# Attention and a feed-forward block on one core: the first images' norms, gelus, convolutions and sums of squares inside the last attention image, and the second image's products ahead of the first maxima

## The reference, cut to what matters

```
h = gelu(rmsnorm2d(x, norm1_w))
x = x + conv1x1(h, conv_w, conv_b)
h = rmsnorm2d(x, norm2_w)
h = gelu(conv1x1(h, ffn_w1, ffn_b1))
x = x + conv1x1(h, ffn_w2, ffn_b2)
```

## Time and profile before

| | us |
|---|---|
| median of 3 runs | 1737.22 (1735.89 to 1737.3) |
| profiled execution, its own time | 1736.72 |
| its span in the trace | 1734.7 |
| PE busy | 1680.9 (97%) |
| DVE busy | 1456.1 (84%) |
| ACT busy | 1368.5 (79%) |
| POOL busy | 337.7 (19%) |
| mean granted TensorE clock | 0.977 |

### The profile page before, as it was taken

How to read it: one execution, slowest core, us unless ns; L and a number is a source line. 1 busy time by engine, 2 the same in 40 slices (tenths; PEclk the granted TensorE clock), 3 DMA queues, 4 the chain that set the end, 5 groups by cost and what they waited for, 6 DMA issues and landing times.

```text
span 1734.7 us, 33327 instructions
## 1 busy us (share of the span) xinstructions
PE 1680.9 (97%) x12402; PEld 677.8 (39%) x12402; DVE 1456.1 (84%) x2414; ACT 1368.5 (79%) x2480; POOL 337.7 (19%) x411
## 2 busy tenths in 40 slices
PE   4999999999999999999999999999999997699999
PEld 2333333333333333333333333333333332355555
DVE  4899999999999999999999999999999991455552
ACT  1288888888888888888888888888888887566664
POOL 4101111111111111111111112121211011322220
PEclk8599999999999999999999999999999998799999
DMA  6133333333333333333333333333333301233332
GB/s 118 24 45 57 56 59 56 59 56 59 54 60 54 60 55 60 55 60 53 61 53 62 53 62 52 50 52 51 51 50 53 51 18 48 87 99 107 105 109 73
DMA packets 58817, 106.17 MB, mean 61 GB/s; under 512 B 33184, under 2 KB 33952, under 8 KB 58656
## 3 DMA queue, kind: packets, MB, share of 16 engines
q1 hardware_dynamic: 56352, 95.66, 32.3%
q10 hardware_dynamic: 2304, 8.39, 1.2%
HBM read 34.48 MB, written 9.06 MB: 25 GB/s over the span
## 4 chain that ended last, share of the span: by engine, by line
PE 91%; DVE 4%; DMA 1%; SPq 1%; POOL 1%; issue 1%; ACT 1%; DVEq 0%; ACTq 0%; POOLq 0%
PE psum L619 30%; PE psum L590 26%; PE psum L603 12%; PE psum L685 6%; PE psum L528 4%; DVE maxes L877 4%; PE psum L657 2%; PE psum L658 2%; PE psum L659 2%; PE psum L565 2%; PE psum L520 2%; PE psum L702 1%; DMA k_stack<-k_low 0%; POOL rms_out L500 0%; PE psum L540 0%
## 5 line engine op out<-in xcount | busy, mean ns | idle before, releaser
L877 DVE TENSOR_REDUCE maxes<-psum 128x1 f32<-128x512 f32 x2048 | 1277.4, 683 | 107.7 <-PE psum L590 105.6
L794 ACT ACTIVATE probs<-psum 128x512 f32<-128x512 f32 x2048 | 1109.3, 597 | 194.0 <-PE psum L603 168.9
L590 PE MATMUL psum<-k_stack,q_stack 62*128 62x512 f32 x2048 | 772.3, 458 | 8.3 <-DMA k_stack<-k_low 4.7
L603 PE MATMUL psum<-q_stack,k_stack 64*128 64x512 f32 x2048 | 752.9, 451 | 1.0 <-ACT probs L794 0.9
L619 PE MATMUL psum<-probs,values 128*32 128x256 f32 (+1 forms) x6912 | 620.2, 431 | 0.5 <-ACT probs L794 0.5
L590 PEld LDWEIGHTS psum<-k_stack,q_stack 62*128 62x128 f32 x2048 | 317.2, 188 | 523.6 <-DVE maxes L877 434.8
L603 PEld LDWEIGHTS psum<-q_stack,k_stack 64*128 64x128 f32 x2048 | 305.0, 185 | 14.3 <-ACT probs L794 9.0
L619 PEld LDWEIGHTS psum<-probs,values 128*32 128x32 f32 x6912 | 136.1, 108 | 310.6 <-issue 231.1
L417 POOL CAST parts<-neg_max 128x16 fp32r<-128x16 f32 x64 | 12.7, 198 | 534.9 <-DVE neg_max L856 534.9
L685 PE MATMUL psum<-probs,inv_den 128*128 128x512 f32 x256 | 116.5, 598 | 0.0
L803 ACT ACTIVATE probs<-psum,params_sb 128x512 f32<-128x512 f32 x128 | 82.2, 686 | 20.9 <-PE psum L659 14.8
(11 more groups left out here) (82 smaller groups left out, 998.2 us busy)
## 6 DMA issues: line engine op xcount, KB each, us to landing
q_stack<-q_high SPq DMA_DIRECT2D x128, 128.0 KB, 3.7
k_stack<-k_high SPq DMA_DIRECT2D x128, 128.0 KB, 5.2
x_sb<-in_x SPq DMA_DIRECT2D x16, 512.0 KB, 7.0
q_stack<-q_low SPq DMA_DIRECT2D x64, 128.0 KB, 6.3
k_stack<-k_low SPq DMA_DIRECT2D x64, 128.0 KB, 7.0
q_stack<-rows SPq DMA_DIRECT2D x512, 2.0 KB
attn<-raw SPq DMA_DIRECT2D x128, 64.0 KB, 2.3
inv_den<-inv_den_rows SPq DMA_DIRECT2D x128, 64.0 KB, 2.3
```

What stands on the lines that cost most here:

```text
L590: nc.tensor.matmul(psum[:, BANKS + tile % BANKS, :], q_stack[used, place, p, chunk % 4, chunk // 4, :], k_stack[used, place, p, HALF * key ...
L603: nc.tensor.matmul(psum[:, tile % BANKS, :], k_stack[used, place, p, 128 * chunk:128 * chunk + 128], q_stack[used, place, p, :, t, :], sta ...
L794: nc.scalar.activation(probs[:, tile % 8, :], psum[:, tile % BANKS, :], ACT.Exp, scale=SCALE).then_inc(probs_ready, 1)
L877: nc.vector.tensor_reduce(maxes[:, chunk // 4, j, 4 * p + chunk % 4, key_half:key_half + 1], psum[:, BANKS + max_tile(u, s, k) % BANKS, :] ...
```

## The change

- **Start.** PE makes all four q and k products and both value pieces of an image in one go (`prologue_image`), for the first and for the second image ahead of unit 0's maxima, in `FIRST_BANKS`. The group mean waits for the value copies. DVE makes the low parts of the first image (`first_rests`), which POOL made.
- **Breaks.** `has_job` makes a step broken only where there is a job.
- **Unit 30** (image 15, first half): POOL squares images 0 and 1, PE sums them at step 5 in bank 7, ACT copies the sums; SP loads all layer 1 weights and spreads the norms of images 0 and 1 (chain 0).
- **Unit 31.** `lead_in(0)` after step 4: norms 1 of images 0 and 1, splits of `wconv` and `w1`, their four gelus. PE convolves image 0 in step 5. `lead_in(1)` after step 6: sums of images 2 and 3, convolution of image 1. `lead_in(2)` after step 9: sums of the convolved images 0 and 1, then norm 1 of image 2 and norm 2 of image 0 on DVE. `lead_in(3)` after the last weighing: denominators of image 15, gelu and split of image 2.
- **After it.** `refine(0)` has its own order: hidden(0,0), convolution of image 2, hidden(0,1), sums, both down products. The projection of image 15 follows it (`project_last`, banks 3 and 4). `refine(1)` to `refine(15)` keep theirs.
- Storage: separate `sums`, `first_weights` for four small weights and later `w2`, a DRAM row pair for each of the first chains.

The core of the diff, common part and run:

```diff
-LAST_PROJ = (0, 15)
+
+
+FIRST_SUMS, FIRST_CONV = (0, 5), (1, 5)
+CHAINS = 3
+
+FIRST_BANKS = ((0, 1, 2, 3), (0, 1, 2, 6))
+PROLOGUE = len(FIRST_BANKS)
...
-            return {None: range(STEPS), 0: range(2), 1: range(2, 7), 2: range(7, 13), 3: range(13, STEPS)}[part]
...
+            return {None: range(STEPS), 0: range(5), 1: range(5, 7), 2: range(7, 10), 3: range(10, STEPS)}[part]
 
         def qk_bank(c, n):
-
-            return psum[:, n, :] if c == 0 else misc
...
+        def prologue_image(b, half, s):
+
+            return b + 2 if half == 1 and s == 2 and 0 <= b + 2 < PROLOGUE else None
...
+        def run(eng, slot, lead_in, refine, project_last=lambda: None):
...
             slot(IMAGES - 1, 1, 0)
-            for part in range(2):
+            for part in range(3):
                 slot(IMAGES - 1, 1, 1, part)
-            refine(-4)
-            slot(IMAGES - 1, 1, 1, 2)
-            refine(-3)
+                lead_in(part)
...
             slot(IMAGES - 1, 1, 1, 3)
             slot(IMAGES, 0, 0, 0)
-            activate(-3)
...
+            lead_in(3)
             refine(0)
...
+            project_last()
+            for c in range(1, IMAGES):
                 refine(c)
```

SP and POOL:

```diff
+                if half == 0 and b == IMAGES - 1:
+                    sp.dma_start(wconv[:, :], d["wconv"]).then_inc(ffn_weights_in, 16)
+                    sp.wait_ge(split_done, 2 * IMAGES)
+                    sp.dma_start(w1, d["w12"][:, 0:HIDDEN]).then_inc(ffn_weights_in, 16)
+                    sums_in(0)
+                if half == 0 and has_image(b - 1) and part is None:
+                    denominators(b - 1)
+                if half == 0 and b == IMAGES - 1:
+                    rms_rows(0)
+                    sp.wait_ge(pv_done, (u - 1) * STEPS + STEPS)
+                    sp.wait_ge(scores_ready, u * TILES)
+                    spread(0, 0, inv_rms1, inv1_in)
+                    spread(0, 1, inv_rms2, inv2_in)
+                    sp.dma_start(w2, d["w12"][:, HIDDEN:2 * HIDDEN]).then_inc(ffn_weights_in, 16)
...
+            def lead_in(part):
+                if part == 1:
+                    sums_in(1)
+                    rms_rows(1)
+                    sp.wait_ge(normed1_ready, 1)
+                    spread(1, 0, inv_rms1, inv1_in)
+                if part == 2:
+                    sums_in(2)
+                    rms_rows(2)
+                    sp.wait_ge(normed1_ready, 2)
+                    spread(2, 0, inv_rms2, inv2_in)
+                if part == 3:
+                    sp.wait_ge(normed1_ready, 3)
+                    spread(1, 1, inv_rms1, inv1_in)
+                    sp.wait_ge(normed2_ready, 1)
+                    spread(2, 1, inv_rms2, inv2_in)
+                    denominators(IMAGES - 1)
...
+                if c == 0:
+                    return
...
+                if half == 0 and b == IMAGES - 1:
+                    pool.wait_ge(split_done, 2 * IMAGES)
+                    pool.wait_ge(v_ready, 2 * IMAGES)
+                    square_of(0, square1)
+                    square_of(1, square2)
...
+                if half == 0 and b == IMAGES - 1:
+                    inverse_rms(0)
...
+            def lead_in(part):
+                if part == 0:
+                    pool.wait_ge(sums_ready, 1)
+                    square_of(2, square1)
+                    square_of(3, square2)
+                if part in (1, 2):
+                    inverse_rms(part)
+                if part == 3:
+                    normalise(IMAGES - 1)
...
```

PE:

```diff
+                if b == IMAGES - 1 and (half, s) == FIRST_SUMS:
+                    pe.wait_ge(ffn_setup, 3)
+                    pe.wait_ge(proj_taken, (b - 1) * NT)
+                    pe.wait_ge(first_squares, 2)
+                    sum_squares(square1, square2, 7)
...
+                if prologue_image(b, half, s) is not None:
+                    pe.wait_ge(hid_ready, c + 1)
+                    at_least(pe, qk_full, c * 4)
+                    for n in range(4):
+                        qk_product(c, n)
+                    at_least(pe, gn_var, c + 1)
+                    values_of(c, 0)
+                    pe.wait_ge(v_full, c * 2 + 1)
+                    values_of(c, 1)
+                if half == 1 and s in QK_STEPS and c >= PROLOGUE and has_image(c):
...
+            def has_job(b, half, s):
+                at = (half, s)
+                if at in (LAST_K, *VALUES):
+                    return PROLOGUE <= b + 1 < IMAGES or at == FIRST_SUMS and b == IMAGES - 1
+                if at in (GROUP_MEAN, GROUP_VAR):
+                    return has_image(b + 2)
+                if at in PROJ:
+                    return 0 < b < IMAGES
+                return half == 1 and s in QK_STEPS and PROLOGUE <= b + 2 < IMAGES
...
-                    broken = s in SIDE_STEPS[half] or b == IMAGES and (half, s) == LAST_PROJ
+                    broken = has_job(b, half, s)
+                    if b == IMAGES - 1 and (half, s) == FIRST_CONV:
+                        for k in range(3):
+                            scores(u, 2 * parity + half, s, k)
+                        weigh_before(u, parity, half, s, 0, HALF)
+                        pe.wait_ge(max_taken, UNITS * TILES)
+                        pe.wait_ge(weights_split, 1)
+                        convolve(0, 0)
+                        convolve(0, 1)
+                        scores(u, 2 * parity + half, s, 3)
+                        continue
                     middle = 2 if s % NK == 1 and not broken else 1
...
-                        if k == 1 and broken:
+                        if k == 1 and (broken or b < 0):
...
+            def lead_in(part):
+                if part == 1:
+                    pe.wait_ge(first_squares, 4)
+                    pe.wait_ge(sums_taken, 1)
+                    sum_squares(square1, square2, SUMS_BANK)
+                    convolve(1, 0)
+                    convolve(1, 1)
+                if part == 2:
+                    pe.wait_ge(sums_taken, 2)
+                    pe.wait_ge(conv_squares, 2)
+                    sum_squares(square1, square2, SUMS_BANK)
...
+                if c == 0:
                     pe.wait_ge(weights_split, 2)
                     pe.wait_ge(probs_ready, UNITS * TILES)
+                    pe.wait_ge(proj_taken, (IMAGES - 1) * NT)
+                    hidden(0, 0)
+                    convolve(CONV, 0)
+                    convolve(CONV, 1)
+                    hidden(0, 1)
+                    sums_of(0)
                     pe.wait_ge(acc_taken, UNITS * NT)
+                    pe.wait_ge(ffn_weights_in, 48)
+                    down(0, 0)
+                    down(0, 1)
+                    return
+                if c == 1:
                     pe.wait_ge(proj_taken, IMAGES * NT)
...
+            def project_last():
+                b = IMAGES - 1
+                pe.wait_ge(attn_ready, b + 1)
+                pe.wait_ge(conv_taken, (CONV + 1) * NT)
+                for t in range(NT):
+                    nc.tensor.matmul(psum[:, CONV_BANKS[t], :], wp[:, :], attn[:, HALF * t:HALF * t + HALF],
+                                     start=True, stop=True).then_inc(proj_ready, 1)
...
```

ACT, then DVE:

```diff
+                if prologue_image(b, half, s) is not None:
+                    for n in range(4):
+                        take_qk(b + 2, n)
+                    for part in range(2):
+                        take_values(b + 2, part)
...
+                if b == IMAGES - 1 and (half, s) == FIRST_SUMS:
+                    act.wait_ge(sums_ready, 1)
+                    act.wait_ge(pv_done, u * STEPS)
+                    nc.scalar.copy(sums, misc).then_inc(sums_taken, 1)
...
+            def lead_in(part):
+                if part == 0:
+                    activate(0)
+                    activate(1)
...
+            def refine(c):
+                if c == 0:
+                    activate(CONV)
+                    gelu_hidden(0, 0)
+                    square_in_front(0)
+                    square_behind(0)
+                else:
+                    square_in_front(c)
+                    store(c - 1)
+                    square_behind(c)
                     gelu_hidden(c, 0)
-                if has_image(c + FIRST - 1) and not is_first(c + FIRST - 1):
-                    activate(c)
-                if has_image(c):
-                    gelu_hidden(c, 1)
+                    if has_image(c + FIRST - 1):
+                        activate(c + FIRST - 1)
+                gelu_hidden(c, 1)
+                if c == 0:
+                    activate(FIRST - 1)
...
+                if b == -2 and half == 1 and s == 15:
+                    first_rests(0, q_full, q_high, q_low)
+                    first_rests(1, k_full, k_high, k_low)
...
+            def lead_in(part):
+                if part == 0:
+                    dve.wait_ge(stack_in, UNITS * (16 * STACK_DMAS))
+                    dve.wait_ge(added, 2 * NT)
+                    norm_in_front(0)
```

(24 more changed lines are left out.)

362 lines of the change are left out of this document (182 added, 180 removed).

## The result

| kernel | median, us | lowest to highest | executions |
|---|---|---|---|
| before | 1737.26 | 1735.89 to 1737.68 | 4 |
| with the change | 1713.83 | 1712.49 to 1714.98 | 4 |

What follows compares the result with a forecast made beforehand. The prediction took the kernel as PE-bound except for two holes, at the start and late. Terms -2.0 - 1.5 + 7.2 - 23.2 = -19.5 against 1736.7 gave 1717.2, plus 0.5 for the median: 1717.7 us, range 1710 to 1727.

Steps and rivals of the forecast that it cites:

- A: Start: second image's products and value pieces moved before the first maxima; -2.0 us, bounds +1 and -4.
- C: Last unit: table loads, gelus, convolutions and sums added on ScalarE and PE; +7.2 us, bounds +5 and +11.
- B: Units 29 and 30: jobless steps no longer broken, first sum of squares added; -1.5 us, bounds -3 and +1.
- D: From the last attention matmul to `refine(1)`: reordered work shortens this stretch; -23.2 us, bounds -25 and -20.
- moving the two rests ... nothing: Start: moving the splits' low parts from GpSimd to VectorE gains nothing, as PE no longer waits for the stacks.
- the wait for the rows of maxima: Start: first scores would newly wait for the rows of maxima to land; +1.2 us.
- The -3.5 for the jobs that leave the first slot: Slot 0: one product (counted 1.5 us) and two value pieces at 1.0 each go; -3.5 us.
- Rival 2: Start gives nothing: first maxima at 42 and the rows late; 1719.7 to 1720.7 us, chance 0.15.
- Rival 1: Last unit: clock holds in the gelu gap, and units 29 and 30 give their bound; 1715 us, chance 0.2.
- Rival 5: Last unit: clock falls in the gelu gap and stays down until `refine(1)`, so slower; 1746 us, chance 0.03.
- Rival 3: Last unit: table switches have a drain beside the load, 2.8 us more; 1720.5 us, chance 0.08.
- Rival 4: A chain of norms is late, or PE waits inside the last unit; 3 to 5 us, 1721 to 1723, chance 0.1.

Runs made afterwards that it cites:

- rests_back: The changed kernel with the low parts of the first image's q and k formed on GpSimd again instead of VectorE; median 1717.92 us.
- breaks_back: The changed kernel with steps broken by their number again, whether or not they have a job; median 1719.98 us.
- change_again: The changed kernel run once more with nothing edited; median 1715.30 us.
- swap: The changed kernel with VectorE splitting the third gelu output ahead of the reciprocal of the last denominators; median 1710.49 us.
- all3: The changed kernel with GpSimd's later squares, twelve useless matmuls before the first convolution, and the third gelu's split ahead of the last reciprocal; median 1709.76 us.
- two_more_loads: all3 plus one unused single-column gelu on ScalarE in the last unit, forcing one more pair of table switches; median 1712.85 us.

## Why the prediction was right, and where it was not

The sum was right within its range, and a good part of that is luck: two errors of opposite sign met. A gave 5.2 more than forecast, beyond its bound of -4, and C cost 3.2 more. The mechanisms of B and D held. Of the 3.9 us between forecast and median, 2.2 are the sum's (-21.7 for -19.5), 0.5 was added for a median above the profiled execution, and 1.2 is that here the profiled execution was the slowest of its four.

**A: -2.0 forecast, -7.2 measured.** Three steps of it failed. First, "moving the two rests ... nothing": GpSimd, not SP, is what the second image's norm waits for once its products stand in front; rests_back prices it at 2 to 3 us. The prediction looked at the stacks, for which TensorE no longer waits, and not at what else stands behind the rests on their engine. Second, the wait for the rows of maxima, +1.2, isn't there: first maxima to first score is 31.74, all of it VectorE's pace (53 maxima at 0.60). Third, the unbroken steps of units 0 and 1, 1.6 to 3 us by breaks_back, were counted nowhere. The products and value pieces cost less than I took (5.39 for 6.8; the granted clock was back before 33), which gives the rest of the 3.0 us by which the first maxima came before 40.5. The -3.5 for the jobs that leave the first slot looks right only because it stands beside that third error: from the first score to unit 28 the change has -4.2, but breaks_back, where the jobs are gone and the breaks stay, has -2.1 (1254.1 for 1256.2).

Rival 2, that the start gives nothing, did not come: the first maxima stood at 37.5, not 42, and the rows were no wait.

**B: -1.5, measured -1.2.** Both terms hold: the breaks -1.7 (forecast -2.4), the first sums and their neighbours +0.6 (forecast +0.9). No wait for rows was seen in the last unit, but the cover that the prediction gave it was wrong: SyncE, said to be through 9 us ahead of them, was through at 1401.4, waited 2.2 for VectorE's transpose (1403.37) and issued the rows at 1403.60. More than 2.2 us of further work ahead of them on SyncE would have delayed the rows.

**C: +7.2, measured +10.4 and, in change_again, +7.9.** The loads and gelus are 6.5 (+6.4 forecast). TensorE's extra block is paid as ScalarE idle: 4.3 us at full clock in all3 for the 3.5 of before, +0.8 where the prediction had +2.3, +0.9 and -3.4, so -0.2. The contention of squares and norms, 0.5 to 0.7, stood nowhere. The clock is the rest: priced at 1.0, it costs nothing in some executions and 2.5 in others, like this one. Rival 1 (the clock holds) didn't come in either profile of this kernel, though its result in time is that of a short fall. Rival 5 is refuted as a lasting state: the longest fall was 10.2 us.

**D: -23.2, measured -24.0.** The steps came where the prediction had them: convolution 2 at T+8.9 (T+9.1), its idle 4.44 (about 5), the reciprocal at T+7.2, released as said, `refine(1)` at T+27.1 (T+27.9). swap shows that the named cause of the wait is the cause. The forecast also had the clock down behind it, as it was here.

Rival 3, the drain beside a table load, is refuted by the two loads of the change shown above and by the pair in two_more_loads, 2.80 with its gelu. The Trainium skill (ScalarE: Activation LUTs, What ACT_TABLE_LOAD costs) has 2.66 for one switch. Here the measurement decides, 1.28 to 1.30. Rival 4 didn't come: the last norm's chain was done at T+1.3.
